# Conditioned attention on one core: who issues the first weights, how many zero products run ahead, and how many products of V precede the first maxima

## The reference, cut to what matters

```python
def _L0_cond_ref(x, tokens, Wq, bq, Wk, bk, Wv, bv):      # x (8, 512, 512), tokens (8, 1, 512)
    Q = _split_heads(x @ Wq.T + bq)                       # 16 heads of 32
    K = _split_heads(x @ Wk.T + bk)
    V = _split_heads(x @ Wv.T + bv)
    tQ = _split_heads(tokens @ Wq.T + bq)
    tK = _split_heads(tokens @ Wk.T + bk)
    scores = jnp.einsum('bhqd,bhkd->bhqk', Q + tQ, K + tK) / jnp.sqrt(jnp.float32(HEAD_DIM))
    attn = jax.nn.softmax(scores, axis=-1)
    out = jnp.einsum('bhqk,bhkd->bhqd', attn, V)
    return out.transpose(0, 2, 1, 3).reshape(B, S, D_MODEL)
return x + _L0_cond_ref(x, cond_1024[:, None, :], Wq, bq, Wk, bk, Wv, bv)
```

## Time and profile before

| | us |
|---|---|
| median of 3 runs | 660.39 |
| lowest, highest run | 660.14, 661.38 |
| the profiled execution, its own time | 662.08 |
| its span, first to last instruction | 660.3 |
| PE busy in it | 652.3 |
| DVE busy | 540.8 |
| POOL busy | 485.9 |
| ACT busy | 373.4 |

### The profile page before, as it was taken

The page is one execution under the profiler, slowest core; times in us unless marked ns, Lnnn a source line. Parts: engine busy times, 40 slices in busy tenths (PEclk is TensorE's granted clock), DMA queues, the critical chain, the costliest instruction groups (busy, mean ns, idle before and its releaser), DMA issues.

```text
span 660.3 us, 10095 instructions
## 1 busy us (share of the span) xinstructions
PE 652.3 (99%) x3556; PEld 444.4 (67%) x3556; DVE 540.8 (82%) x819; ACT 373.4 (57%) x659; POOL 485.9 (74%) x202
## 2 busy tenths in 40 slices
PE   8999999999999999999999999999999999999997
PEld 5776776666776666776666776666776666676442
DVE  4586888888888888888888888888888888887887
ACT  6335565555665555665555665555655555555673
POOL 5519677789777789777779777779777778766890
PEclk9999999999999999999999999999999999999999
DMA  8934335554334554334554434554334544336401
GB/s 289 222 87 101 92 91 132 144 145 111 107 95 123 145 144 114 107 99 117 145 145 118 109 98 113 143 146 122 105 102 107 145 129 113 82 93 150 130 18 64
DMA packets 48278, 79.87 MB, mean 121 GB/s; under 512 B 9826, under 2 KB 9826, under 8 KB 48226
## 3 DMA queue, kind: packets, MB, share of 16 engines
q1 hardware_dynamic: 47700, 79.21, 44.5%
q10 hardware_dynamic: 528, 0.02, 0.0%
HBM read 19.95 MB, written 8.39 MB: 43 GB/s over the span
## 4 chain that ended last, share of the span: by engine, by line
PE 93%; DVE 4%; DMA 1%; SPq 1%; ACT 0%; issue 0%
PE bank L291 26%; PE bank L395 19%; PE bank L415 17%; PE bank L374 17%; PE bank L351 13%; DVE mf L700 3%; DMA Pt<-xT 1%; PE bank L446 1%; SPq L960 0%; PE bank L324 0%; DMA Qs<-mt 0%; PE bank L423 0%; PE bank L336 0%; SPq L935 0%; DVE bank L700 0%
## 5 line engine op out<-in xcount | busy, mean ns | idle before, releaser
L610 ACT ACTIVATE Pt<-bank 128x512 f32<-128x512 f32 x512 | 299.6, 600 | 227.7 <-PE bank L395 156.0
L700 DVE TENSOR_REDUCE mf<-bank 128x1 f32<-128x512 f32 x496 | 333.4, 686 | 73.6 <-PE bank L374 70.6
L887 POOL TENSOR_TENSOR A<-A,Pt 128x2048 f32<-128x2048 f32 x59 | 270.8, 4589 | 4.6
L395 PE MATMUL bank<-Qs,Ks 98*128 98x512 f32 x496 | 199.0, 403 | 0.6 <-ACT Pt L610 0.5
L374 PE MATMUL bank<-Ks,Qs 96*128 96x512 f32 x496 | 198.1, 399 | 0.4 <-DVE mf L700 0.3
L887 POOL TENSOR_TENSOR A<-Pt 128x2048 f32<-128x2048 f32 x30 | 138.4, 4612 | 2.8 <-DVE part_sums L725 2.0
L395 PEld LDWEIGHTS bank<-Qs,Ks 98*128 98x128 f32 x496 | 93.3, 188 | 50.9 <-ACT Pt L610 27.5
L415 PE MATMUL bank<-Pt,V 128*32 128x512 f32 x1024 | 119.1, 596 | 0.1
L857 POOL TENSOR_TENSOR Xl<-xr,Xh 128x512 fp32r<-128x512 f32 x28 | 36.1, 1289 | 112.7 <-ACT Xh L573 112.7
L374 PEld LDWEIGHTS bank<-Ks,Qs 96*128 96x128 f32 x496 | 93.8, 189 | 27.7 <-DVE mf L700 5.0
L291 PE MATMUL bank<-Xh,Wh 128*128 128x512 f32 x256 | 102.3, 400 | 0.8 <-ACT Xh L565 0.8
(11 more groups left out here) (70 smaller groups left out, 374.7 us busy)
## 6 DMA issues: line engine op xcount, KB each, us to landing
Qs<-hi SPq DMA_DIRECT2D x60, 256.0 KB, 3.6
Ks<-hi SPq DMA_DIRECT2D x60, 256.0 KB, 3.6
Qs<-lo SPq DMA_DIRECT2D x30, 256.0 KB, 4.1
Ks<-lo SPq DMA_DIRECT2D x30, 256.0 KB, 3.2
xr<-xT SPq DMA_DIRECT2D x28, 256.0 KB, 2.7
res<-xT SPq DMA_DIRECT2D x28, 256.0 KB, 2.9
outT<-ot SPq DMA_DIRECT2D x28, 256.0 KB, 3.2
Qs<-mt SPq DMA_DIRECT2D x124, 4.0 KB
```

Source lines behind the costliest of these rows:

```text
L395: e.matmul(st_bank(u)[:, :], k[0:98, j, kc * P:(kc + 1) * P], q[0:98, j, :], start=True, stop=True).then_inc(t_st, 1)
L610: e.activation(exponentials(g)[:, kc, j, :], st_bank(u)[:, :], ACT.Exp, scale=SCALE).then_inc(a_e, 1)
L700: e.reduce_max(to[:, 4 * j + qc:4 * j + qc + 1], MXB[u % 2][:, :], AXX).then_inc(v_mx, 1)
L887: e.tensor_tensor(sums, ex[:, 0, :, :] if kc == 1 else sums, ex[:, kc, :, :], ALU.add).then_inc(p_a, 1)
```

## The change

ACT issues the DMA of Wq's part 0, as its first instruction and ahead of the DMA of `cT`; SP issues x's four chunks one behind the other and no longer that weight load. One zero product of 256 columns goes (4 become 3), and the two of 64 columns move from behind the first `condition` to ahead of it. Nine products of V instead of seven run ahead of the first maxima, and three products per maxima begin one step later (23 for 22).

```diff
-WARM, WARM_MORE, V_AHEAD, MORE_AT = 4, 2, 7, 22
+WARM, WARM_MORE, V_AHEAD, MORE_AT = 3, 2, 9, 23
...
                 for i in range(WARM):
                     e.matmul(MXB[0][:, 0:256], res[:, 0:P], res[:, 0:256], start=True, stop=True)
-
-            def warm_up_more():
                 for i in range(WARM_MORE):
                     e.matmul(MXB[0][:, 0:64], res[:, 0:P], res[:, 0:64], start=True, stop=True)
...
             warm_up()
             condition(0, 0)
-            warm_up_more()
             for n in range(12):
                 project_qk(0, 0, n)
...
+            e.dma_start(wraw[0][:, 0, :], wdram[0][0]).then_inc(d_w[0][0], 16)
             e.wait_ge(v_c, 1)
             e.dma_start(cT[:, :, 0:B], condT).then_inc(d_c, 16)
...
-            load_x0(0)
-            w(0, 0)
-            for kc in range(1, KC):
+            for kc in range(KC):
                 load_x0(kc)
```

## The result

| | before | changed |
|---|---|---|
| median, us (9 runs each) | 660.88 | 663.59 |
| lowest, highest | 660.14, 662.99 | 662.38, 665.45 |
| profiled execution, us | 662.08 | 663.09 |
| its span | 660.3 | 661.3 |

The changed kernel takes 1.0039 of the time before, 95% interval 1.0023 to 1.0056: 2.7 us slower by the medians, where 0.3 us less was forecast. The two profiled executions differ by only 1.0 us.

A forecast was written before the change was run, and what follows sets the result against it. PE's own work sets the pace from 22 us on, so only the start can move: -0.2 to -1.2 us against the profile, -0.4 to +0.3 against the 660.39 median, together 0.3 gained: 660.1 us, range 658.9 to 661.6.

The forecast's parts named there:

- The condition behind the weights: ACT's queue at the start: the condition's load delayed behind the weights by 0 to 0.8 us, 0.3 taken.
- PE's clock is late: Rival: PE idle up to 1 us before the condition, first projection at 1.2 GHz; 1.2 to 2.4 us later, chance 0.13.
- The odd chunk: x's chunk 3 lands 1.6 us oddly late, likelier a profile accident; rival that it goes whole: 658.8 to 659.5, chance 0.22.
- V ahead: Two more products before the first maxima: +0.47 us on the end, or nothing if the maxima wait for K's stack.
- The zero products: PE's zero work ahead of the condition ends 0.05 to 0.5 us earlier; first product behind the condition 0.44 earlier.
- The first product: PE's start of the first projection, 5.83 before: moves by between -0.44 and 0 us, -0.2 taken.

The follow-up runs named there:

- dma_w6: dma_alone with six large zero products instead of four; 661.58 us, 1.0011 of the kernel before.
- dma_alone: The kernel before with only the two loads changed (weights ahead of the condition on ACT, x's four chunks one behind the other on SP); 663.29 us.
- after_w5: The changed kernel with five large zero products instead of three; 662.25 us, 1.0016 of the kernel before.
- no_dma_part: The changed kernel with the two loads put back as before, zero products and V's products as changed; 661.39 us, 1.0004 of the kernel before.
- cond_late_w6: cond_late with six large zero products instead of four; 662.52 us, 1.0029 of the kernel before.
- zeros_alone: The kernel before with only the zero products changed: three large instead of four, the two small ones ahead of the condition; 661.19 us, ratio 1.0003.
- v9_alone: The kernel before with only nine products of V ahead of the first maxima, three per maxima from step 23; 661.25 us, ratio 1.0006.
- v5_alone: The kernel before with five products of V ahead of the first maxima instead of seven, three per maxima from step 21; 661.21 us, ratio 1.0007.
- warm1: The kernel before with one large zero product instead of four, all loads untouched; 662.51 us, 1.0021 of the kernel before.
- cond_late: The kernel before with ACT loading its table and copying one column before it issues the condition's DMA; 664.38 us, ratio 1.0049.
- cond_on_sp: The changed kernel with the condition's DMA issued by SP between x's chunks 0 and 1; 662.03 us, 1.0014 of the kernel before.
- rows_zeros: The kernel before with the condition loaded in whole 512-byte rows and the zero products as changed; 660.92 us, ratio 0.9994.
- rows_after: The changed kernel with the condition padded and loaded in 128 rows of 512 bytes, without the clearing of `cT`; 662.06 us, 1.0011 of the kernel before.

## Why the prediction was wrong

**The condition behind the weights: the term that failed.** The prediction bounded its delay in the queue by 0 and 0.8 us and took 0.3, from the distance of two large landings. The landing moved by 1.57 us (1.21 + 5.0 for 1.04 + 3.6), 0.17 of it by the later issue and 1.4 by the slower landing; in the other three profiles with this order the second part was 0.8 (dma_w6), 1.0 (dma_alone) and 1.8 (after_w5). The row used was one of 256 KB loads; the condition is 512 packets of 32 bytes, and no row before showed such a load behind a large one. What makes it so late stays open: the old order has it late too at times (5.1 in no_dma_part).

**The clock: the right mechanism with too small a chance.** The rival "PE's clock is late" named the place, the idle time of PE before the condition ("up to 1 us"; it was 1.56), and 1.2 to 2.4 us of loss. It had a chance of 0.13, because it leaned on a delay that had been mis-sized. The measured 2.7 us lie a little beyond it. In the profiled execution the clock was not late but fell back behind the gap (0.50 granted from 8 to 10 us); in dma_alone it was late. The chance was also argued from the amount of zero work ("but for 0.5 us"), and 0.5 us of zero work was not small: more of it takes back 1.3 us in after_w5 and 1.7 in dma_w6. Whether the zero work must reach the condition is not settled, since in cond_late_w6 it did not and the clock held. The slots of 0.467 that the prediction took for the low clock measure 0.43 (3.78 us for eight records, 2.93 for six), a detail that changes nothing.

**The odd chunk: right in the main.** The prediction held that the late chunk 3 (5.8 us) was in part an accident of that execution and that the median runs lacked it. That profile lay 1.2 us over its kernel's median; the profiles of zeros_alone and v9_alone, with the loads as before, show their roundings of chunk 3 0.7 to 0.8 earlier, its landing at 5.0 us for 5.8, PE's wait for it down from 1.0 to 0.2 at most, and V's products at 21.3 for 22.04. So there was little for the contiguous chunks to gain.

**V ahead: the chain right in the profile, its price not shown.** The first maxima moved by the start of V's products plus two slots, PE's wait at the first scores grew from 0.19 to 0.66 as forecast, and the chain kept its length. By the times 0.4 us fits and so does none, and in the other direction (v5_alone) nothing came back.

**The zero products: right in the start, not in what follows.** The first product came earlier without the load's change (5.52 in zeros_alone for 5.83), but the first slots were 0.43 and the ninth product came 0.5 later. The main sum had no term for that; it put the clock into the rival alone. The times show neither gain nor loss.

**The first product** was put at 5.4 to 5.8 and was at 6.63. The range, 658.9 to 661.6, ended where the clock's case began. With the first product 0.8 later (6.63 for 5.83), V ahead's 0.47 and the clock's 1.3 to 1.7, added to the 660.39 from which the prediction counts, the sum would be 663.0 to 663.4; that is an estimate, and it takes each part to pass on whole. Of the 3.5 us between the forecast 660.1 and the measured 663.59, 0.5 is the base: the kernel before has 660.88 in nine runs, for 660.39 in three.

## What to carry to other kernels

A small load of many little packets that gates the first real work is a risk: lay it out in whole rows, and don't put it second behind a bulk load on its queue without a profile that shows when it lands. The distance between bulk landings is no bound for how late it can be. Nor is one profile enough, since the landing varied between executions with the loads unchanged. Work that only keeps TensorE busy is part of the start's timing and not waste: with two large zero products added, 1.3 of the changed kernel's 2.7 us and 1.7 of dma_alone's 2.3 came back with the loads unchanged. And before a profile is used as the base, place its execution among the runs: here it was 1.2 us over the median, and most of the wait that the change was to mend (1.0 us of PE's time) was in that one.

## What the runs showed of the hardware

- The condition's DMA, 16 KB in 32-byte pieces, took 3.4 to 6.6 us from issue to landing. With its issue at 1.04 and nothing ahead of it on its queue it took 3.4 to 3.7 us in four profiles and 4.3, 4.5 and 5.1 in three others (warm1, v5_alone, no_dma_part); behind the weights 4.4 to 5.4; issued at 1.32 in cond_late and cond_late_w6 6.6 and 6.2. In 512-byte rows the same data took 3.1 and 3.2 us first on the queue and 3.9 and 4.1 behind the weights.
- TensorE ran with the granted clock at 0.50 (1.2 GHz) from 8 to 10 us after an idle gap of 1.56 us that followed 3.4 us of work. After a gap of 1.46 us that followed 4.8 us of work (cond_late_w6) it stayed at 1.00, with slots of 0.23.
- The column shows 1.00 at the very start, where the slots of the zero products are 0.43 us per 256 columns and tell 1.2 GHz: the first rise has to be read from slots. By them it moved with zero products and gaps, and also without: three large and two small zero products and no gap behind them left the projection's first slots at 0.43 in zeros_alone and cond_on_sp and at 0.23 to 0.34 in rows_zeros (which starts its zero products 0.14 us earlier).
- The lower clock in the first projection went with 1.3 to 1.9 us of 661 in four pairs (after_w5, dma_w6, warm1's 1.5, and cond_late_w6, whose 1.9 holds some 0.4 of an earlier landing). cond_on_sp and rows_after took back as much, 1.6 and 1.5 us, by when the condition lands.
